# Second stage of a vision tower: attention output product and second gating product with full fp32 operands in place of halves

## What is computed

```
comp = softmax(concat([qv, out]) @ Ws.T + bs, over the value heads)
out  = (comp * out).sum(over the value heads)     # "att" in the kernel
out  = res + out @ Wf.T + bf                      # attention output product
on   = layernorm(out) * g2 + b2
ffn  = relu(on @ Wr1.T + br1) @ Wr2.T + br2       # first and second gating product
return out + ffn
```

## Time and profile before

| what | value |
|---|---|
| time, median of 3 runs | 629.18 us (626.67 to 630.38) |
| the profiled execution | 628.95 us |
| its span from the first to the last instruction | 627.1 us |
| mean granted TensorE clock | 0.916 |
| TensorE busy | 534.4 us |
| VectorE busy | 384.8 us |
| ScalarE busy | 277.2 us |
| GpSimd busy | 189.4 us |

### The profile page before, as it was taken

How to read it: one execution, slowest core, us unless ns; L and a number is a source line. 1 busy time by engine, 2 the same in 40 slices (tenths; PEclk the granted TensorE clock), 3 DMA queues, 4 the chain that set the end, 5 groups by cost and what they waited for, 6 DMA issues and landing times.

```text
span 627.1 us, 12120 instructions
## 1 busy us (share of the span) xinstructions
PE 534.4 (85%) x3932; PEld 449.0 (72%) x3932; DVE 384.8 (61%) x961; ACT 277.2 (44%) x639; POOL 189.4 (30%) x258
## 2 busy tenths in 40 slices
PE   2798999999997855778899999999998759479996
PEld 2577888888886643557788888888887647358886
DVE  3346544656446643256978887888777751268884
ACT  3022132322323323236686777677777750234342
POOL 3231233322332100443355335434632110122321
PEclk9598999999998966779999999999998868569999
DMA  8503422444223000000000000000000000000000
GB/s 334 202 12 147 157 72 86 156 156 156 103 83 127 2 2 0 0 1 0 2 1 3 1 0 0 0 0 0 0 1 1 2 0 1 0 1 23 15 22 21
DMA packets 7677, 29.61 MB, mean 47 GB/s; under 512 B 1824, under 2 KB 3040, under 8 KB 5216
## 3 DMA queue, kind: packets, MB, share of 16 engines
q1 hardware_dynamic: 7648, 29.23, 12.5%
HBM read 27.98 MB, written 1.25 MB: 47 GB/s over the span
## 4 chain that ended last, share of the span: by engine, by line
PE 40%; DVE 9%; issue 5%; ACT 3%; DVEq 1%; POOL 1%; POOLq 0%; ACTq 0%
PE score L1465 7%; PE bz L1252 3%; PE tb L1252 3%; PE score L1307 3%; PE tb L1254 3%; PE tb L1253 3%; PE bz L1254 2%; PE bz L1253 2%; PE bank L1253 2%; PE bank L1254 2%; PE bank L1252 2%; DVE o L1052 2%; PE bz L1266 1%; PE tb L1266 1%; DVE we_h L1206 1%
## 5 line engine op out<-in xcount | busy, mean ns | idle before, releaser
L310 POOL TENSOR_TENSOR small<-small,half 114x1 f32<-114x1 f32 x44 | 24.8, 564 | 211.4 <-DVE small L743 183.0
L360 POOL TENSOR_TENSOR h<-h,scaled 114x256 f32 (+1 forms) x88 | 64.5, 732 | 39.1 <-ACT scaled L609 33.0
L1354 PE MATMUL bz<-ebuf 128*128 128x256 f32 x256 | 60.0, 388 | 0.2 <-DVE cb L891 0.2
L1325 PE MATMUL tb<-cst,p_exp 114*114 114x114 f32 x352 | 46.6, 276 | 13.4 <-issue 5.6
L483 ACT ACTIVATE p_exp<-sc,cst 114x608 f32<-114x608 f32 x66 | 48.1, 794 | 18.6 <-DVE sc L820 18.6
L491 ACT ACTIVATE pt<-tb 114x456 f32<-114x456 f32 x66 | 35.3, 557 | 41.9 <-PE tb L1325 41.9
L1325 PEld LDWEIGHTS tb<-cst,p_exp 114*114 114x114 f32 x352 | 37.6, 141 | 22.5 <-issue 8.4
L1354 PEld LDWEIGHTS bz<-ebuf 128*128 128x128 f32 x256 | 48.5, 195 | 6.7 <-DVE cb L891 0.4
L609 ACT ACTIVATE scaled<-bank,gl 114x256 f32<-114x256 f32 x88 | 39.2, 471 | 28.3 <-DVE gl L997 14.7
L1465 PE MATMUL score<-v,pt 114*114 114x137 f32 x352 | 49.3, 283 | 0.0
L1465 PEld LDWEIGHTS score<-v,pt 114*114 114x114 f32 x352 | 44.0, 179 | 2.1 <-issue 0.3
(11 more groups left out here) (218 smaller groups left out, 1443.0 us busy)
## 6 DMA issues: line engine op xcount, KB each, us to landing
ebuf<-in_w_in SPq DMA_DIRECT2D x8, 1024.0 KB, 4.9
ebuf<-in_w_out SPq DMA_DIRECT2D x8, 1024.0 KB, 6.9
x_raw<-in_x_tiles SPq DMA_DIRECT2D x11, 342.0 KB, 6.8
raw<-in_w_c SPq DMA_DIRECT2D x1, 1952.0 KB, 8.1
raw<-in_w_a SPq DMA_DIRECT2D x2, 768.0 KB, 6.1
out<-h SPq DMA_DIRECT2D x10, 114.0 KB
ebuf<-in_fc SPq DMA_DIRECT2D x1, 1024.0 KB, 4.9
ebuf<-in_proj SPq DMA_DIRECT2D x1, 1024.0 KB, 7.0
```

The costliest lines, as they stand in the source:

```text
L360: gp.tensor_tensor(h[0:R, t, :], h[0:R, t, :], scaled[0:R, e % 4, :], ALU.add).then_inc(moe_acc, 1)
L1325: last = pe.transpose(tb[g % 2][0:R, i * R:(i + 1) * R], p_exp[0:R, 4 * g + i, :], cst[0:R, CI:CI + R])
L1354: last = pe.matmul(bz[:, m * D:(m + 1) * D], ebuf[:, 0, c * D + m * P:c * D + (m + 1) * P], ebuf[:, 1, c * D:(c + 1) * D], start=(c == 0), ...
```

## The change

- The weights of the output product and of the second gating product are no longer split. They come by transfers of their own into `wf` and `wr2` and are used there as fp32. The one transfer of `w_c` becomes four, and who waits for it waits for 64 instead of 16.
- What GpSimd splits into `wc` is shorter: 2368 columns in eight parts of 296, where it was 3904 in parts of 488. The first gating product's weights move to `C_R1S` in it.
- The transposed `att` is copied whole by ScalarE into a tile of its own, `attT`; VectorE's low half of it goes, and TensorE waits for ScalarE's copy. The output product is two matmuls instead of six.
- ScalarE's high half (`c3_hi`) and VectorE's low half (`c3_relu`) of the relu go. TensorE waits for the four relu instructions and does four matmuls instead of twelve. The relu's own wait moves from `relu_lo` to `wr2_mm` of the tile before.
- The order of everything else in all streams stays.

The diff, cut to its core:

```
 C_QK, C_V, C_G, C_F, C_R1, C_R2, C_END = ...
-CHUNK = C_END // E
+SPLIT = C_F + C_R2 - C_R1
+C_R1S = C_F
+CHUNK = SPLIT // E
...
-        wc = sb("wc", [P, 2, C_END], F32R)
+        wc = sb("wc", [P, 2, SPLIT], F32R)
+        wf = sb("wf", [P, DC * D])
+        wr2 = sb("wr2", [P, 4 * D])
...
+        attT = sb("attT", [P, DC, R])
...
-            sp.dma_start(raw[:], w_c).then_inc(wc_in, 16)
+            sp.dma_start(raw[:, 0:C_F], w_c[:, 0:C_F]).then_inc(wc_in, 16)
+            sp.dma_start(raw[:, C_R1S:SPLIT], w_c[:, C_R1:C_R2]).then_inc(wc_in, 16)
+            sp.dma_start(wf[:], w_c[:, C_F:C_R1]).then_inc(wc_in, 16)
+            sp.dma_start(wr2[:], w_c[:, C_R2:C_END]).then_inc(wc_in, 16)
...
             def c3_att(t):
-                turn_hi(t3, xth[2], two(bz[:, 0:2 * R]), t, (wr1_mm, t))
+                turn_hi(t3, attT, two(bz[:, 0:2 * R]), t, (wf_mm, t))
...
             def c3_relu(t):
                 act.wait_ge(r1T_mm, t + 1)
-                since(act, relu_lo, t)
+                since(act, wr2_mm, t)
...
-            def c3_hi(t):
-                act.wait_ge(relu_32, 4 * t + 4)
-                since(act, wr2_mm, t)
-                act.activation(rh[:], r32.rearrange("p (j r) -> p j r", j=4), ACT.Copy).then_inc(relu_hi, 1)
...
-            def c3_att(t):
-                turn_lo(t3, xth[2], xtl[2], two(bz[:, 0:2 * R]), t)
...
-            def c3_relu(t):
-                dve.wait_ge(relu_hi, t + 1)
-                V.tensor_tensor(rl[:], r32.rearrange("p (j r) -> p j r", j=4), rh[:].bitcast(F32), ALU.subtract).then_inc(relu_lo, 1)
...
             def c3_wf(t):
-                pe.wait_ge(t3["lo"], t + 1)
-                product(bz[0:R, 256:512], xth[2], xtl[2], wc, C_F, D, (0, D)).then_inc(wf_mm, 1)
+                pe.wait_ge(t3["hi"], t + 1)
+                for c in range(DC):
+                    last = pe.matmul(bz[0:R, 256:512], attT[:, c, :], wf[:, c * D:(c + 1) * D], start=(c == 0), stop=(c == DC - 1))
+                last.then_inc(wf_mm, 1)
...
             def c3_r2(t):
-                pe.wait_ge(relu_lo, t + 1)
+                pe.wait_ge(relu_32, 4 * t + 4)
                 for j in range(4):
-                    o = C_R2 + j * D
-                    last = mm3(bz[0:R, 0:D], rh[:, j, :], rl[:, j, :], wc[:, 0, o:o + D], wc[:, 1, o:o + D], j == 0, j == 3)
+                    last = pe.matmul(bz[0:R, 0:D], r32[:, j * R:(j + 1) * R], wr2[:, j * D:(j + 1) * D], start=(j == 0), stop=(j == 3))
```

More of the change, by code:

```diff
@@ L179, in vit_tower @@
         y4 = x_raw[:, 4 * R:6 * R].rearrange("p (c r) -> p c r", c=DC)
-        rh = xs[:, 0, 0:4 * R].rearrange("p (j r) -> p j r", j=4)
-        rl = xs[:, 1, 0:4 * R].rearrange("p (j r) -> p j r", j=4)
         fct = wa[:, 0, 0:DC * HID].rearrange("p (c n) -> p c n", c=DC)
@@ L219, in vit_tower @@
             "qk1_mm v1_mm qk1_out qkT1_mm v1_ready pv1_mm pv1_out mix_step mix_exp x1_kept")
-        wf_mm, r2_ready, h_r2, wr1_mm, wr1_out, r1T_mm, relu_hi, relu_32, relu_lo, wr2_mm, res1 = sems(
-            "wf_mm r2_ready h_r2 wr1_mm wr1_out r1T_mm relu_hi relu_32 relu_lo wr2_mm res1")
+        wf_mm, r2_ready, h_r2, wr1_mm, wr1_out, r1T_mm, relu_32, wr2_mm, res1 = sems(
+            "wf_mm r2_ready h_r2 wr1_mm wr1_out r1T_mm relu_32 wr2_mm res1")
         tern, tern_mm, fc_mm, gelu, g_stat, g_rstd, gT_mm, gT_hi, gT_lo, bw_ready, lnw_split, pw_ready, centred = sems(
@@ L342, in _ @@
             rstd(nA, 1)
-            gp.wait_ge(wc_in, 16)
+            gp.wait_ge(wc_in, 64)
             a_step(1, True, True)
@@ L657, in c_step @@
                     c2_pt(i - 2, (0,))
-                if on[4]:
-                    c3_hi(i - 4)
                 if on[2]:
@@ L864, in prep_products @@
             def prep_products():
-                dve.wait_ge(wc_in, 16)
+                dve.wait_ge(wc_in, 64)
                 dve.wait_ge(vec_in, 16)
@@ L1084, in c_step @@
                     gate(i - 1, 6)
-                if on[4]:
-                    c3_att(i - 4)
                 if on[1]:
@@ L1132, in c_step @@
                     gate(i, 3)
-                if on[4]:
-                    c3_relu(i - 4)
                 if on[3]:
@@ L1482, in c3_r1 @@
                 pe.wait_ge(t4["lo"], t + 1)
-                product(bz[0:R, :], xth[2], xtl[2], wc, C_R1, 2 * D, (0, 2 * D)).then_inc(wr1_mm, 1)
+                product(bz[0:R, :], xth[2], xtl[2], wc, C_R1S, 2 * D, (0, 2 * D)).then_inc(wr1_mm, 1)
             def c3_r1T(t):
```

## The result

The changed kernel takes 622.92 us, the median of 11 runs, against 629.18 for the kernel before (11 runs on the same chip, 625.42 to 631.57). The ratio is 0.9894, with a 95% interval of 0.9862 to 0.9926: faster by 1.06%, twice the 0.5% that a measurement tells. The ratio is that of nine runs, 618.25 to 627.05 us: two slow runs, of 628.80 and 1056.97 us, are left out of it, and what made the last so long no trace shows. The forecast of 627.7 stood inside "no change", and the result lies under its range.

The account below looks back on a forecast made before the run. TensorE was taken to bound the loop, the latency of one tile's chain the last turns. Terms +0.1 (step 4), -1.2 (loop), +0.6, -0.2, -0.7 (steps 11 to 14) sum to -1.4: 627.7 us, range 624.5 to 631.5.

Parts of the forecast that it names:

- The price of a full product in place: Second gating product: 8 records of 0.217 us, 1.74 instead of 1.51, +0.23 at the high clock.
- The relu's wait: Loop, before the second gating product: a stall of 0.59 us goes, and the product ends 0.36 earlier.
- the four transfers: First stage: weights loaded by four transfers instead of one; set at nothing, upper end 1 us.
- Rivals 2 and 3: Full products dearer on TensorE: the first 0.47 us each, total +1.0, chance 0.06; the second 0.29 per record, +8.5, chance 0.07.
- The turn: Each of six loop turns gets shorter by 0.2 us, -1.2 in all.
- what is late next is the transpose of `x2`: Loop, after the second gating product: with the subtraction gone, its input comes 0.3 us ahead of need.
- the attention output product: Loop: 0.87 us instead of 0.81, and a dearer first matmul behind it, +0.14 a turn.
- The tail: Steps behind the loop: +0.6 us for 11 and 12 together, -0.2 for 13, -0.7 for 14.
- steps 11 and 12: Behind the loop: ScalarE's copy goes, -0.5 each; product at 1.2 GHz +0.77; taken with the output product as +0.6 together.
- rival 4: Last four turns: shorter waits leave two second gating products at the high clock, -3.4, total -4.8, 624.2 us; chance 0.13.
- Rival 1: Loop: `x2` comes no earlier, so each turn costs +0.14 instead of -0.2; total +0.6, 629.6 us; chance 0.12.
- Rival 5: Second gating product still waits for something of VectorE: all prices, no gain, +6.2, 635.2 us; chance 0.02.

Follow-up runs that it names:

- e3: Kernel before, with the relu written rounded as high half and used for both halves, copy and subtraction left out, twelve matmuls kept: 619.57 us, ratio 0.9871.
- e4: Changed kernel with VectorE's subtraction put back in its old queue place, its result unread, only the next relu waiting for it: 627.9 us, ratio 0.9964.
- e2: Kernel before, with the second gating product alone on full operands and the relu's halves gone; output product keeps its halves: 623.28 us, ratio 0.9889.
- e7: Changed kernel with ScalarE's copy of the relu put back in its old queue place, nothing on TensorE waiting for it: 623.59 us, ratio 0.9925.
- e1: Kernel before, with the attention output product alone on full operands; second gating product keeps its halves: 628.9 us, ratio 0.9989.

## Why the prediction was wrong

The sum said -1.4 us; the medians say -6.3.

*Right.* The price of a full product in place: 8 records in 1.73 us (1.74 forecast). The relu's wait was the bound and goes; 0.59 was its size, and in e3 the turn falls by 0.61. The stretch from the transposes at 413.47 of the earlier trace rows to the `x2` transpose is shorter by 0.30 (0.36 forecast). The first stage: GpSimd's step after its split starts at 51.65 instead of 51.56, with 8.95 us of idle ahead, so the shorter split costs nothing. For the four transfers that isn't settled: the second stage begins at 248.2 to 249.6 us (mean 248.7) in the five profiles of kernels with one transfer of `w_c`, and at 247.3 to 252.1 (mean 249.9) in the nine with several. The cost may be near the 1 us that the prediction had as its upper end. Rivals 2 and 3 fell with the 0.217. The Trainium skill, page "FP8 and Floating Point Precision", section "TensorE Precision Notes", counts four passes for a true FP32 product; the trace has two records of 0.217 for it, 0.43 and not 4 x 0.1175 = 0.47.

*The turn: -0.39 instead of -0.2.* Two terms were mis-sized. First, "what is late next is the transpose of `x2`": I gave its earlier input no price of its own. In before `x2` ended only 0.1 us ahead of its transpose, which cost something although no idle stood there (I read it as a drained pipeline): the stretch from this transpose to the attention's lasts 1.75 in before, 1.60 in after, 1.80 in e3 and e4, where `x2` is late. That is -0.15. Second, the attention output product came to +0.06 instead of +0.14 against the kernel before (e2 shows the 0.13 on top of the other part). Together -0.30 - 0.15 + 0.06 = -0.39.

*The tail: -5.9 instead of -0.3 for steps 11 to 14.* This is the step that failed. I took each low stretch of before as given and charged the full products double in it (+0.77 in steps 11 and 12 each, +0.86 in step 13). But a low stretch isn't a place in the program. With both kernels at 1.00 the same steps bring -2.4, of it 1.17 up to step 13's product and 1.23 from there to step 14's; the forecast's own terms at the high price give 0.97 (1.3 of copy, subtraction and hand-over, less 0.23 and 0.1 of the products) and, with the 0.3 of the attention's low half, 1.27. So the waits were sized about right, and the products' price at 1.2 GHz was mostly not paid. In the profiles of e4 (which also keeps the subtraction) and e2, where the products of steps 13 and 14 did pay it, the tail is only 0.4 and 1.2 us shorter than before's. With the clock held, loop and tail bring 4.7 us, which by itself puts the time at the lower edge of the range. The other 3.5 us in the traces are rival 4, to which I gave 0.13: the clock came back ahead of the second gating product of steps 13 and 14. I named that case, but not what would bring it about, and the runs don't show it either. The tail lies 5.6 us under its sum, where rival 4 had 3.4, since it priced the product alone; the sums of step 13 (4.67 to 3.62) and the transposes ahead of the relu (1.02 to 0.61) are faster too. Steps 11 and 12, from step 10's product to step 12's, take 40.35 us instead of 40.48, forecast +0.6: step 11's product runs at the high level now, 1.73 where 2.65 stood.

*Rival 1* didn't happen: the subtraction goes from ahead of `x2`, and e4 shows what it costs when it doesn't. *Rival 5* fell: L1483 waits for ScalarE alone.

*What the medians add.* Loop -2.3 and tail -5.9 are -8.2 by the traces, while the medians differ by 6.3. The head, longer by 0.6 us in the mean of after's three executions than in before's, takes part of that back: the second stage begins 1.2 us later in after's three, by chance or by the transfers. And two of the three profiles of before have a mean granted clock of 0.916, where the 38 runs of it beside the experiments have 0.925; the profiles of after have 0.939, 0.931 and 0.934, and its nine runs 0.935. So the traces make the clock's share look larger than the runs do.

*What stays open.* In after's three executions the clock comes back earlier, and holding it in both kernels takes away part of the difference. What makes it come back is not shown, and shorter waits alone don't: e2, e4 and e7 have the same waits and, in one profile each, tails of 88 to 90 us and 12 to 14 us at the low level between the products of steps 13 and 14 (14.8 in before, 3.4 in after); e3 has 10, e1, with the old wait, 14.7. e7 differs from after by a single ScalarE copy. The mean granted clocks over all their runs are 0.927 (e2), 0.929 (e4) and 0.931 (e7), between before's 0.925 and after's 0.935. Nor can the runs tell the clock's share of the gain from scatter: without it 4.7 us were left, a ratio of 0.9925, just inside the interval measured for the change.

## What to carry to other kernels

Before costing a change in a part where the granted clock falls, price it twice: at the high clock throughout, and with the clock as it is; the stretches at half clock need not stay where they were. Here the tail brought 2.4 us with the clock held and 5.9 without, and kernels with the same waits got less. Here an operand that was ready within 0.1 us of its use cost 0.15 to 0.2 us though no idle showed, and an operation ahead of it in its engine's queue cost as if it were on the path (e4). If TensorE waits in such a part, matmuls that nobody reads, put ahead of the waits, are worth trying first: here they brought more than the change.

## What the runs showed of the hardware

- A record of a full product (256 columns) takes 0.217 us at 2.4 GHz and doubles at 1.2 GHz: in e7, 8 records and their drain take 3.76, where 3.42 and the drain were estimated.
- 58 matmuls that nobody reads, in the tail, made the kernel before 1.3% faster by the runs; in the profiles its tail is 7.8 us shorter, 1.2% of the span. The Trainium skill, page "TensorE: Matmul & The Clock Gate", section "Part 1: The HAM clock gate (the "warmup" mystery)", puts what the ramp at a kernel's start costs under 1% of a typical kernel's span, and says that it varies from run to run. That the place varies the traces bear out: in the first stage one and the same product ran at the high level in one execution of after (1.92 us) and at the low one in two others (3.54). Here the clock falls many times after the start, and what that costs in the tail alone is over 1%.
- With the same wait of 1.18 us ahead, the second gating product ran at the high level for all of its length (after, step 13), for a part (after, step 14) and not at all (e2, steps 13 and 14; e7, step 14).
